# Adjacency masks of a four-layer graph kernel: cast by GpSimd's transfers instead of by ScalarE

## The chip, the cores and the metric

The kernel runs on one core of one Trainium2 chip. The time is the device time of one execution in microseconds. The kernel before has a median of 260.65 us over 3 runs (260.47 to 260.87). The core has five engines that follow their own instruction lists and meet at semaphores: TensorE (PE, with its weight loads shown as PEld), VectorE (DVE), ScalarE (ACT), GpSimd (POOL) and SyncE (SP), which here only issues transfers.

## The reference, cut to what matters

There are 32 graphs of 256 nodes with 128 features each. `adj` is int32 with values 0 and 1 only; it is symmetric and has a full diagonal.

```python
x = _layernorm(x + _L0_gnn_ref(x, adj, W0, a_src, a_dst))   # attention
x = _layernorm(x + _L1_gnn_ref(x, adj, W1, a))              # attention
x = _layernorm(x + _L2_gnn_ref(x, adj, a0, a1, a2, a3, bias))
x = _layernorm(x + _L3_gnn_ref(x, adj3, adj, weight, bias))
# L0 and L1: h = x W^T;  e = leaky_relu(s_i + d_j, 0.2), masked where adj == 0
#            out = softmax(e) h
# L2: alpha = sigmoid(leaky(x a_r x^T)) where adj == r + 1, else 0;  out = alpha x + bias
# L3: out = sum_r (adj == r + 1) x W_r + bias
```

With values 0 and 1 the relation of layers 2 and 3 is always the first one, so one mask per graph serves all four layers. The kernel notes on the way whether a value other than 0 and 1 occurs (step `seen`) and would then compute everything again on a general path, which does not run with these inputs.

## The kernel before

**Units of work.** Two graphs make a pair; there are 16 pairs, numbered 0 to 15. Every step works on one pair. A tile has 128 partitions; a graph's 256 nodes are two blocks of 128.

**Steps of a pair.** Layers 0 and 1 (the digit stands behind the step's name): `h` projects x on TensorE, `logits` copies two columns on VectorE, `gains` and `v` are exponentials on ScalarE, `dT`, `peak`, `top` and `dmax` find the largest logit of the pair, `rows` spreads the gains along rows on TensorE, `weight` (L857) makes the attention weights on VectorE and multiplies them by the mask, `vals` scales the values on ScalarE, `out` aggregates on TensorE, `rsum`, `rinv` and `res` divide and add the residual on VectorE. `stats` (L907), `var`, `pow` (L541, always on GpSimd) and `norm` make the layer norm; in layer 1 `center` stands between. Layer 2: `xT2` transposes on TensorE and is copied on ScalarE, `xTa` is the same tile scaled by a feature vector (on GpSimd at L565 or on ScalarE at L645), `score` is their product, `sigmoid`, `umax` and `alpha` turn it into weights (alpha multiplies by the mask, L865), then `out2`, `res2` (L888) and the norm. Layer 3: `high` and `low` split x in two f16 parts, `agg` multiplies them by the mask on TensorE, `out3` multiplies by the centred weights, then `res3`, `stats3`, `var3`, `pow3`, `norm3` and the store. `bias` (L536) adds the centred bias to x ahead of `res2` and `res3`.

**Masks before.** SyncE loads the int32 adjacency of a pair into one of four places (`adj_all`, ADJ = 4). ScalarE casts each graph to bf16, times EDGE = 0.5 (`make_mask`, L609), into one of ten places (`mask_all`, MASK = 10), and reads the int32 tile again in `seen` (L601), which takes the square of the value less 0.5 and sums it. The factor 0.5 is wanted by layer 2 (tanh instead of a sigmoid) and is taken out of layer 3 by doubling the centred weights (L762). A load of adjacency waits until the mask and the `seen` of the pair four before it are done.

**Order.** The order of each engine's steps is written out by hand in the table `ORDER`, as pairs `step:pair`, one string per engine ("sp" for SyncE). Where a step can run on two engines, it runs on the one whose string names it (`doer`). `BANKS` gives the bank of PSUM of each product. Engines are in order, so a step that waits holds all behind it. Tiles are rings with a depth in pairs (X_IN 4, XT_IN 3 for the loads of x and its transpose). Step `centre` on VectorE centres weights and biases. In the profile `w_pack` is the first weight matrix with the vectors of all layers beside it.

## Time and profile before

| | us |
|---|---|
| median of 3 runs | 260.65 (260.47 to 260.87) |
| the profiled execution | 259.62 |
| its span in the profile | 257.1 |
| TensorE matmuls busy | 228.6 |
| VectorE busy | 226.5 |
| ScalarE busy | 206.5 |
| GpSimd busy | 173.6 |
| HBM read, written | 17.17 MB, 4.19 MB |

Busy time is the time in which at least one instruction of the engine runs, so it is below the number of instructions times their mean duration where instructions overlap. In the rows further down a group has its busy time first and the mean duration of one instruction behind it. "L857" is a line of the kernel; the name left of the arrow is written, the names right of it are read. "idle before" is time in which the engine stood still just before such an instruction, with the instruction that ended the wait. PEclk is the clock of TensorE that was granted, 1.00 being all of it; DMA is the busy share of the 16 transfer engines.

### The profile page before, as it was taken

How to read it: one execution, taken by the hardware profiler on the slowest of the kernel's cores; microseconds unless marked ns; L12 is line 12 of the kernel's file. 1: busy time of each engine (PE TensorE's matmuls, PEld its weight loads, DVE VectorE, ACT ScalarE, POOL GpSimd, SP SyncE). 2: the span in 40 equal slices, each digit the busy share in tenths (PEclk: the TensorE clock that was granted, in tenths of full speed). 3: DMA queues.
4: the chain of work that ended last, by engine and by line, in shares of the span. 5: the costliest groups of instructions: out<-in, count | busy, mean ns of one | idle time of the engine just before them, and what ended most of it. 6: DMA issues, size and time to landing. Idle time of an engine off the chain costs nothing.

```text
span 257.1 us, 5794 instructions
## 1 busy us (share of the span) xinstructions
PE 228.6 (89%) x1745; PEld 207.1 (81%) x1745; DVE 226.5 (88%) x794; ACT 206.5 (80%) x634; POOL 173.6 (67%) x248
## 2 busy tenths in 40 slices
PE   6869898998988999999999999999999988989670
PEld 6769788986977999879898888898979877887560
DVE  0498999989998999989999999999989998998851
ACT  3797999986867999878359965986895959989874
POOL 1003031759789988697357999867596876799892
PEclk9999999999999999999999999999999997999995
DMA  6997538400020444111142000101100011110113
GB/s 243 402 387 213 209 92 259 166 18 0 1 85 0 126 124 134 71 41 46 41 125 82 3 1 0 42 4 51 34 0 3 3 42 42 42 41 0 43 41 129
DMA packets 12145, 21.77 MB, mean 85 GB/s; under 512 B 1104, under 2 KB 5968, under 8 KB 12112
## 3 DMA queue, kind: packets, MB, share of 16 engines
q1 hardware_dynamic: 11824, 21.24, 24.9%
q8 instruction: 15, 0.25, 0.4%
q10 hardware_dynamic: 288, 0.14, 0.2%
q14 instruction: 18, 0.15, 0.2%
HBM read 17.17 MB, written 4.19 MB: 83 GB/s over the span
## 4 chain that ended last, share of the span: by engine, by line
PE 35%; DVE 23%; ACT 19%; POOL 13%; issue 6%; DMA 1%; POOLq 0%; DVEq 0%; ACTq 0%
PE banks L1176 13%; PE banks L1116 6%; POOL frstd L541 6%; DVE wgt_all L857 5%; DVE fstats L907 5%; PE banks L1143 4%; ACT odd_square L601 4%; POOL fxTa L565 4%; ACT xs_all L678 3%; PE banks L1173 3%; PE banks L1153 3%; DVE fres_all L899 3%; ACT wgt_all L651 3%; PE banks L1133 2%; ACT vals_all L636 2%
## 5 line engine op out<-in xcount | busy, mean ns | idle before, releaser
L541 POOL TENSOR_TENSOR frstd<-fvar,minus_half 128x4 f32<-128x4 f32 x64 | 65.1, 1020 | 36.5 <-ACT fvar L684 29.3
L1176 PE MATMUL banks<-vals_all,wgt_all 128*128 128x129 f32 x512 | 64.0, 279 | 3.4 <-issue 2.5
L1176 PEld LDWEIGHTS banks<-vals_all,wgt_all 128*128 128x128 f32 x512 | 60.6, 194 | 5.1 <-issue 3.1
L857 DVE SCALAR_TENSOR_TENSOR wgt_all<-banks,gain,mask_all 128x256 f32<-128x256 f32 x128 | 52.7, 471 | 1.9 <-PE banks L1133 1.9
L536 POOL TENSOR_TENSOR xb_all<-xs_all,bias_cen 128x256 f32<-128x256 f32 x64 | 45.5, 736 | 8.7 <-ACT xs_all L678 4.0
L907 DVE BATCH_NORM_STATS2 fstats<-fres_all 128x6 f32<-128x256 f32 x128 | 47.8, 417 | 0.5
L678 ACT ACTIVATE xs_all<-fres_all,frstd 128x128 f32<-128x128 f32 x124 | 39.5, 399 | 6.1 <-POOL frstd L541 6.0
L1143 PE MATMUL banks<-fxT,fxTa 128*128 128x256 f32 x128 | 31.3, 386 | 1.8 <-DVE wgt_all L865 0.6
L1176 PE MATMUL banks<-xs_all,wgt_all 128*128 128x128 f32 x256 | 31.4, 276 | 0.4 <-DVE wgt_all L865 0.4
L1176 PEld LDWEIGHTS banks<-xs_all,wgt_all 128*128 128x128 f32 x256 | 29.9, 192 | 0.9 <-DVE wgt_all L865 0.4
L565 POOL TENSOR_SCALAR fxTa<-fxT,w_pack 128x256 f32<-128x256 f32 x28 | 25.6, 930 | 6.4 <-ACT fxT L616 6.4
L1143 PEld LDWEIGHTS banks<-fxT,fxTa 128*128 128x128 f32 x128 | 22.6, 190 | 6.0 <-issue 1.6
L616 ACT COPY fxT<-banks 128x256 f32<-128x256 f32 x64 | 20.4, 382 | 5.7 <-PE banks L1101 4.6
L888 DVE TENSOR_TENSOR fres_all<-banks,xb_all 128x512 f32<-128x512 f32 x32 | 21.6, 678 | 3.4 <-PE banks L1173 3.1
L651 ACT ACTIVATE wgt_all<-banks 128x512 f32<-128x512 f32 x32 | 19.2, 600 | 6.5 <-PE banks L1143 6.4
L821 DVE TENSOR_TENSOR banks<-banks,wgt_all 128x512 f32<-128x512 f32 x32 | 21.0, 688 | 1.4 <-ACT banks L652 1.3
L1153 PE MATMUL banks<-mask_all,fxTa 128*128 128x256 bf16 x128 | 17.3, 276 | 4.3 <-POOL fxTa L547 2.2
L1133 PE MATMUL banks<-ident,gain 128*128 128x128 f32 x128 | 20.1, 284 | 0.9 <-ACT gain L620 0.8
L609 ACT ACTIVATE mask_all<-adj_all 128x512 bf16<-128x512 int32 x32 | 18.4, 630 | 2.6 <-DMA adj_all<-adj_turned 2.5
L865 DVE SCALAR_TENSOR_TENSOR wgt_all<-banks,mask_all 128x512 f32<-128x512 f32 x32 | 20.4, 677 | 0.0
L1116 PE MATMUL banks<-w_fast,xT_all 128*128 128x130 f32 x128 | 19.8, 307 | 0.5 <-DVE w_fast L750 0.3
L547 POOL TENSOR_TENSOR fxTa<-xs_all,fxTa 128x256 f16<-128x256 f32 x30 | 19.6, 678 | 0.0
(90 smaller groups left out, 421.5 us busy)
## 6 DMA issues: line engine op xcount, KB each, us to landing
adj_all<-adj_turned SPq DMA_DIRECT2D x16, 512.0 KB, 4.1
xT_all<-x_turned SPq DMA_DIRECT2D x16, 256.0 KB, 3.0
x_all<-x_laid SPq DMA_DIRECT2D x16, 256.0 KB, 3.7
out<-xs_all SPq DMA_DIRECT2D x16, 256.0 KB, 2.2
bias<-biases_laid SPq DMA_DIRECT2D x1, 128.0 KB, 7.7
w_pack<-W_and_columns ACTq DMA_DIRECT2D x1, 68.0 KB, 2.8
w_fast<-W_turned ACTq DMA_DIRECT2D x1, 64.0 KB, 3.1
w_nat<-in_L_gnn_W SPq DMA_DIRECT2D x1, 64.0 KB, 7.5
```

The source lines that it names most:

```text
L536: nc.gpsimd.tensor_tensor(xb(u)[:, :, :], xs(u)[:, :, :], bias_cen[:, int(l) - 2, :, :], ALU.add).then_inc(fast_pool[k], 1)
L541: nc.gpsimd.tensor_tensor(frstd[:, int(l), slot(n), :], fvar[:, int(l), slot(n), :], minus_half[:, :, :], ALU.pow).then_inc(fast_pool[k], 1)
L565: nc.gpsimd.tensor_scalar(fxTa(u)[:, :], fxT(u)[:, :], a2[:, 0:1], None, ALU.mult).then_inc(fast_pool[k], 1)
L651: nc.scalar.activation(wgt(u), scored, ACT.Tanh, scale=0.5 * SLOPE)
L678: last = nc.scalar.activation(xs(u)[:, b, :], fres(u)[:, b, :], ACT.Copy, scale=frstd[:, int(l), u, b:b + 1])
L857: last = nc.vector.scalar_tensor_tensor(out=wgt(u)[:, c, :], in0=place(f"rows{l}", u), scalar=gain[:, u, c, 1:2], in1=maskT(u)[:, c, :], o ...
L907: nc.vector.bn_stats(fstats[:, u, :, :].rearrange("p b k -> p (b k)"), fres(u)[:, :, :].rearrange("p b d -> p d b")).then_inc(fast_dve[k], 1)
L1116: last = nc.tensor.matmul(place(f"h{l}", u)[:, b * HC:(b + 1) * HC], (xT_in if l == "0" else fxT)(u)[:, b * P:(b + 1) * P], w_fast[:, int( ...
L1133: last = nc.tensor.transpose(place(f"rows{l}", u)[:, b * P:(b + 1) * P], gain[:, u, b, 0:1].to_broadcast([P, P]), ident[:, :])
L1143: last = nc.tensor.matmul(place("score", u)[:, c * N:(c + 1) * N], fxTa(u)[:, c * P:(c + 1) * P], fxT(u)[:, :], start=True, stop=True)
L1153: last = nc.tensor.matmul(place("agg", u), part(u)[:, c, :], maskT(u)[:, c, :], start=c == 0 and part is hi, stop=c == NB - 1 and part is lo)
L1176: last = nc.tensor.matmul(place(f"out{l}", u)[:, b * width:(b + 1) * width], wgt(u)[:, c, b * P:(b + 1) * P], (vals if l in "01" else xs)( ...
```

## The change

The int32 tiles `adj_all` go. A new step `mask` on GpSimd issues a transfer per pair that reads int32 from HBM and writes bf16 into `mask_all`, which now has 16 places, one for each pair. Each has a semaphore of its own. `seen` reads the bf16 mask. The factor 0.5 goes as well: `res2` multiplies by 0.5 and `res3` by 1.0 in the instruction that adds the bias, and the doubling of the centred weights goes.

Work changes engines by the table: xTa was on GpSimd for 14 pairs and on ScalarE for 14 and 15; now it is on GpSimd for the pairs 0, 2, 4, 6, 8, 10 and 12 and on ScalarE for the other nine. The layer 1 norms were on GpSimd for nine pairs and on ScalarE for seven; now they are ten and six. The bias sums of bias2:1 and bias3:14 are on VectorE; the layer 2 norm of VectorE was pair 11 and is pair 15; low:15 goes from VectorE to GpSimd. All orders and all banks are new.

On GpSimd the start of the program was this (the identity matrix, then variances and the powers of layers 0 and 1 for the first pairs):

```order
L525 AFFINE_SELECT ident<-zero 128x128
L541 TENSOR_TENSOR frstd<-fvar,minus_half 128x4 x2
L571 TENSOR_SCALAR fvar<-fstats 128x4
L541 TENSOR_TENSOR frstd<-fvar,minus_half 128x4
L571 TENSOR_SCALAR fvar<-fstats 128x4
L541 TENSOR_TENSOR frstd<-fvar,minus_half 128x4
L571 TENSOR_SCALAR fvar<-fstats 128x4
L541 TENSOR_TENSOR frstd<-fvar,minus_half 128x4 x2
```

and is now this (the transfers are of all 16 pairs):

```order
L511 AFFINE_SELECT ident<-zero 128x128
L515 DMA mask_all<-adj_turned 128x1024 x16
L560 TENSOR_SCALAR fvar<-fstats 128x4
L530 TENSOR_TENSOR frstd<-fvar,minus_half 128x4
L560 TENSOR_SCALAR fvar<-fstats 128x4
L530 TENSOR_TENSOR frstd<-fvar,minus_half 128x4
L560 TENSOR_SCALAR fvar<-fstats 128x4
L530 TENSOR_TENSOR frstd<-fvar,minus_half 128x4 x3
L525 TENSOR_TENSOR xb_all<-xs_all,bias_cen 128x256 x2
L544 TENSOR_SCALAR xs_all<-fres_all,frstd,fcenter 128x128 x4
```

All transfers stand in front of the first variance and the first power. On ScalarE the start, up to the values of pair 0 and a little on, was this:

```order
L609 ACTIVATE mask_all<-adj_all 128x512 x2
L620 ACTIVATE gain<-logit 128x8
L601 ACTIVATE odd_square,odd<-adj_all,minus_half 128x1024
L626 ACTIVATE vals_all<-logit,minus_dmax 128x4
L609 ACTIVATE mask_all<-adj_all 128x512 x2
L636 ACTIVATE vals_all<-banks,vals_all 128x128 x4
L620 ACTIVATE gain<-logit 128x8
L601 ACTIVATE odd_square,odd<-adj_all,minus_half 128x1024
L620 ACTIVATE gain<-logit 128x8
L609 ACTIVATE mask_all<-adj_all 128x512 x2
```

and is now this (L592 is `seen`, L604 `gains`, L610 `v`, L620 `vals`, L600 the copies of xT1):

```order
L592 ACTIVATE odd_square,odd<-mask_all,minus_half 128x1024
L604 ACTIVATE gain<-logit 128x8 x2
L592 ACTIVATE odd_square,odd<-mask_all,minus_half 128x1024
L604 ACTIVATE gain<-logit 128x8
L610 ACTIVATE vals_all<-logit,minus_dmax 128x4 x2
L620 ACTIVATE vals_all<-banks,vals_all 128x128 x8
L592 ACTIVATE odd_square,odd<-mask_all,minus_half 128x1024
L610 ACTIVATE vals_all<-logit,minus_dmax 128x4
L620 ACTIVATE vals_all<-banks,vals_all 128x128 x4
L592 ACTIVATE odd_square,odd<-mask_all,minus_half 128x1024
L600 COPY fxT_0<-banks 128x256
L600 COPY fxT_1<-banks 128x256
```

`seen` of pair 0 is now the first instruction, `seen` of pair 2 is the third step, and three pairs go side by side. On VectorE, from the first logits to the first residual, it was this:

```order
L830 COPY logit<-banks 128x4 x2
L838 TENSOR_REDUCE top<-banks 4x1
L842 TENSOR_REDUCE minus_dmax<-banks 128x1
L857 SCALAR_TENSOR_TENSOR wgt_all<-banks,gain,mask_all 128x256 x4
L830 COPY logit<-banks 128x4 x4
L857 SCALAR_TENSOR_TENSOR wgt_all<-banks,gain,mask_all 128x256 x4
L838 TENSOR_REDUCE top<-banks 4x1
L872 TENSOR_SCALAR frow<-banks 128x2 x2
L880 RECIPROCAL finv<-frow 128x4
L842 TENSOR_REDUCE minus_dmax<-banks 128x1
L857 SCALAR_TENSOR_TENSOR wgt_all<-banks,gain,mask_all 128x256 x4
L899 SCALAR_TENSOR_TENSOR fres_all<-banks,finv,x_all 128x128 x4
```

and is now this (L805 logits, L813 peak, L817 dmax, L831 weights, L846 row sums, L874 the residual):

```order
L805 COPY logit<-banks 128x4 x4
L831 SCALAR_TENSOR_TENSOR wgt_all<-banks,gain,mask_all 128x256 x4
L813 TENSOR_REDUCE top<-banks 4x1 x2
L805 COPY logit<-banks 128x4 x2
L817 TENSOR_REDUCE minus_dmax<-banks 128x1 x2
L813 TENSOR_REDUCE top<-banks 4x1
L831 SCALAR_TENSOR_TENSOR wgt_all<-banks,gain,mask_all 128x256 x8
L846 TENSOR_SCALAR frow<-banks 128x2 x2
L817 TENSOR_REDUCE minus_dmax<-banks 128x1
L854 RECIPROCAL finv<-frow 128x4
L874 SCALAR_TENSOR_TENSOR fres_all<-banks,finv,x_all 128x128 x4
```

The weights of pairs 2 and 1 moved ahead of the row sums of pair 0, and the logits of pair 1 ahead of the weights of pair 0.

The diff, with the bodies of the tables cut:

```diff
@@ -54,125 +54,122 @@
-X_IN, XT_IN, ADJ, MASK, XS, FXT, FXTA, VALS, WGT, SG, FRES, XB = 4, 3, 4, 10, 6, 7, 5, 6, 7, 2, 9, 5
-EDGE = 0.5
+X_IN, XT_IN, MASK, XS, FXT, FXTA, VALS, WGT, SG, FRES, XB = 4, 3, 16, 6, 7, 5, 6, 7, 2, 9, 5
...
-        "mask:0 gains0:0 seen:0 v0:0 mask:1 vals0:0 gains0:1 seen:1 gains0:2 mask:2 seen:2 v0:1 mask:3 vals0:1 seen:3 "
+        "seen:0 gains0:0 gains0:1 seen:2 gains0:2 v0:0 v0:1 vals0:0 vals0:1 seen:1 v0:2 vals0:2 seen:3 xT1:0 seen:5 "
...
-        "pow0:0 pow0:1 var0:2 pow0:2 var0:3 pow0:3 var0:4 pow0:4 pow1:0 norm1:0 bias2:0 pow0:5 xTa:0 pow1:1 bias2:1 "
+        "mask:0 mask:2 mask:1 mask:3 mask:5 mask:8 mask:15 mask:6 mask:4 mask:11 mask:10 mask:14 mask:7 mask:9 mask:12 "
+        "mask:13 var0:0 pow0:0 var0:1 pow0:1 var0:2 pow0:2 pow1:0 pow1:1 bias2:0 norm1:1 xTa:0 pow1:2 norm1:2 bias2:2 "
...
@@ -217,7 +214,7 @@
 UP_SQUARE = UP * UP
-COUNTS = {"pe": counts("pe", apart=("turn",)), "act": counts("act"), "dve": counts("dve", apart=("centre",)), "pool": counts("pool")}
+COUNTS = {"pe": counts("pe", apart=("turn",)), "act": counts("act"), "dve": counts("dve", apart=("centre",)), "pool": counts("pool", apart=("mask",))}
 def at(engine, name, u):
@@ -322,7 +319,7 @@
         wait_carrier = sb("wait_carrier", [P, K + 1])
         x_all = sb("x_all", [P, X_IN * H, NB, D])
-        adj_all = sb("adj_all", [P, ADJ * H, NB, N], I32)
+        adj_i = sb("adj_i", [P, NB, N], I32)
         xT_all = sb("xT_all", [P, XT_IN * H, N])
         mask_all = sb("mask_all", [P, MASK * H, NB, N], BF16)
         xs_all = sb("xs_all", [P, XS * H, NB, D])
@@ -416,7 +409,7 @@
         w0_turned_in = sem("w0_turned_in")
         weights_in = sem("weights_in")
         biases_in = sem("biases_in")
-        fast_adj_in = [sem(f"fast_adj_in_{q}") for q in range(ADJ)]
+        fast_mask_in = [sem(f"fast_mask_in_{q}") for q in range(TEAMS)]
         fast_xT_in = [sem(f"fast_xT_in_{q}") for q in range(XT_IN)]
         fast_x_in = [sem(f"fast_x_in_{q}") for q in range(X_IN)]
         fast_pe = [sem(f"fast_pe_{k}") for k in range(K)]
@@ -462,13 +455,6 @@
         @block.sync
         def _(sp):
-            def load_adj(l, n, k):
-                if n >= ADJ:
-                    masker = doer("mask", n - ADJ)
-                    sp.wait_ge(signals[masker][(n - ADJ) % K], at(masker, "mask", final(n - ADJ)))
-                    sp.wait_ge(fast_act[(n - ADJ) % K], at("act", "seen", (n - ADJ) * H))
-                sp.dma_start(adj_all[:, pair(n, ADJ), :, :], adj_turned[n]).then_inc(fast_adj_in[n % ADJ], 16)
-
             def load_x(l, n, k):
                 if n >= X_IN:
                     sp.wait_ge(fast_dve[(n - X_IN) % K], at("dve", "res0", final(n - X_IN)))
@@ -525,6 +511,9 @@
             nc.gpsimd.affine_select(out=ident[:, :], in_=zero[:, :], compare_op=ALU.not_equal, fill=1.0,
                                     base=0, pattern=[[-1, P]], channel_multiplier=1).then_inc(ident_set, 1)
             pool.wait_ge(ident_set, 2)
+            def cast_mask(l, n, k):
+                nc.gpsimd.dma_start(mask_all[:, pair(n, MASK), :, :], adj_turned[n]).then_inc(fast_mask_in[n], 16)
+
             def biases(l, n, k):
                 pool.wait_ge(bias_cen_set, 4)
                 normer = doer(f"norm{int(l) - 1}", n)
@@ -594,19 +583,14 @@
             SEEN = [n for step, l, n in order("act") if step == "seen"]
             def note_odd(l, n, k):
-                act.wait_ge(fast_adj_in[n % ADJ], loaded(n * H, ADJ))
-                if SEEN.index(n):
+                act.wait_ge(fast_mask_in[n], 16)
+                if not SEEN.index(n):
+                    act.wait_ge(ident_set, 2)
+                else:
                     m = SEEN[SEEN.index(n) - 1]
                     act.wait_ge(fast_act[m % K], at("act", "seen", m * H))
-                nc.scalar.activation(odd_square[:, :, :, :], adj_all[:, pair(n, ADJ), :, :], ACT.Square, bias=minus_half[:, 0, 0:1],
+                nc.scalar.activation(odd_square[:, :, :, :], mask_all[:, pair(n, MASK), :, :], ACT.Square, bias=minus_half[:, 0, 0:1],
                                      accum_out=odd[:, n:n + 1]).then_inc(fast_act[k], 1)
-
-            def make_mask(l, n, k):
-                if n >= MASK:
-                    act.wait_ge(fast_pe[(n - MASK) % K], at("pe", "agg", final(n - MASK)))
-                act.wait_ge(fast_adj_in[n % ADJ], loaded(n * H, ADJ))
-                for u in graphs(n):
-                    nc.scalar.activation(maskT(u)[:, :, :], adj_in(u)[:, :, :], ACT.Copy, scale=EDGE).then_inc(fast_act[k], 1)
             def copy_xT(l, n, k):
                 act.wait_ge(fast_pe[k], at("pe", f"xT{l}", final(n)))
@@ -758,8 +742,6 @@
             def output_centre():
                 dve.wait_ge(weights_in, 16)
                 center(1, w3_cen[:, :], w3[:, 0, :], w3[:, 0, :], w3_cen_set)
-                dve.wait_ge(w3_cen_set, 1)
-                nc.vector.tensor_scalar(w3_cen[:, :], w3_cen[:, :], 1 / EDGE, None, ALU.mult).then_inc(w3_cen_set, 1)
             def bias_centres():
                 dve.wait_ge(biases_in, 16)
@@ -848,8 +823,7 @@
             def weights(l, n, k):
                 dve.wait_ge(fast_pe[k], at("pe", f"rows{l}", final(n)))
                 if l == "0":
-                    masker = doer("mask", n)
-                    dve.wait_ge(signals[masker][k], at(masker, "mask", final(n)))
+                    dve.wait_ge(fast_mask_in[n], 16)
                     if n >= WGT:
                         dve.wait_ge(fast_pe[(n - WGT) % K], at("pe", "out2", final(n - WGT)))
                 for u in graphs(n):
@@ -885,7 +859,8 @@
                     dve.wait_ge(signals[biaser][k], at(biaser, f"bias{l}", final(n)))
                     dve.wait_ge(fast_pe[k], at("pe", f"out{l}", final(n)))
                     gathered = banks[:, bank_of(f"out{l}", n * H), :].rearrange("p (h b c) -> p h b c", h=H, b=NB)
-                    nc.vector.tensor_tensor(fres_all[:, pair(n, FRES), :, :], gathered, xb_all[:, pair(n, XB), :, :], ALU.add).then_inc(fast_dve[k], 1)
+                    nc.vector.scalar_tensor_tensor(out=fres_all[:, pair(n, FRES), :, :], in0=gathered, scalar={"2": 0.5, "3": 1.0}[l],
+                                                   in1=xb_all[:, pair(n, XB), :, :], op0=ALU.mult, op1=ALU.add).then_inc(fast_dve[k], 1)
                     return
                 for u in graphs(n):
                     if l == "0" and n >= FRES:
@@ -1156,7 +1131,7 @@
             def outputs(l, n, k):
                 if l == "3" and n == first("pe", "out3"):
-                    pe.wait_ge(w3_cen_set, 2)
+                    pe.wait_ge(w3_cen_set, 1)
                 for u in graphs(n):
                     if l in "01" or u % H == 0:
                         bank_free(f"out{l}", u)
```

## Rows read from the trace of the kernel before

**Rows 1.** The page, part 1: busy us, share of the span, instructions

```profile
PE 228.6 (89%) x1745; PEld 207.1 (81%) x1745; DVE 226.5 (88%) x794; ACT 206.5 (80%) x634; POOL 173.6 (67%) x248
```

**Rows 2.** Stages: length, busy us (instructions) of PE, PEld, DVE, ACT, POOL, PEclk, DMA, GB/s

```profile
0.00:33.40 33.40, 27.68 (x187) 25.26 (x188) 21.99 (x102) 25.36 (x68) 3.16 (x11) 1.00 0.79 280
33.40:241.20 207.80, 194.26 (x1511) 176.81 (x1509) 197.93 (x678) 170.32 (x529) 159.35 (x224) 0.99 0.18 55
241.20:257.10 15.90, 6.62 (x50) 4.99 (x50) 6.60 (x16) 10.86 (x38) 11.04 (x15) 0.82 0.20 69
```

**Rows 3.** Waits of VectorE, 33.4 to 241.2 us: releaser, us, times, longest

```profile
DVE minus_dmax L842 <- PE banks L1126: 1.5, 3, 0.8
DVE banks L821 <- ACT banks L652: 1.3, 4, 0.4
DVE fcenter L921 <- POOL frstd L541: 1.3, 3, 0.6
...
DVE fscale L846 <- ACT vals_all L626: 0.4, 1, 0.4
DVE bad L929 <- ACT xs_all L675: 0.4, 1, 0.4
```

**Rows 4.** Groups by line and shape: count, busy us, mean ns, idle before

```profile
L565 POOL TENSOR_SCALAR fxTa<-fxT,w_pack 128x256 f32<-128x256 f32 x28 | 25.6, 930 | 6.4 <-ACT fxT L616 6.4
...
L888 DVE TENSOR_TENSOR fres_all<-banks,xb_all 128x512 f32<-128x512 f32 x32 | 21.6, 678 | 3.4 <-PE banks L1173 3.1 <-PE banks L1176 0.3
...
L865 DVE SCALAR_TENSOR_TENSOR wgt_all<-banks,mask_all 128x512 f32<-128x512 f32 x32 | 20.4, 677 | 0.0
...
L609 ACT ACTIVATE mask_all<-adj_all 128x512 bf16<-128x512 int32 x32 | 18.4, 630 | 2.6 <-DMA adj_all<-adj_turned 2.5
...
L555 POOL TENSOR_SCALAR xs_all<-fres_all,frstd,fcenter 128x128 f32<-128x128 f32 x36 | 15.8, 455 | 5.1 <-DVE fcenter L921 5.1
...
L645 ACT ACTIVATE fxTa<-banks,w_pack 128x256 f32<-128x256 f32 x4 | 1.7, 492 | 0.0
...
L794 DVE TENSOR_TENSOR fxTa<-xs_all,fxTa 128x256 f16<-128x256 f32 x2 | 0.8, 422 | 0.8 <-ACT fxTa L658 0.8
```

**Rows 5.** Timeline, 1 to 21 us: start, us, engine, line, operation

```profile
1.18 0.29 POOL L525 TENSOR_SCALAR_AFFINE_SELECT ident<-zero 128x128 f32<-128x128 f32 x1 [0.20 <-POOL zero L522]
1.20 0.91 SPq L470 DMA_DIRECT2D adj_all<-adj_turned  x2
...
4.86 2.10 PE L1116 MATMUL banks<-w_fast,xT_all 128*128 128x130 f32 x8 [0.32 <-DVE w_fast L750]
5.42 1.15 ACT L609 ACTIVATE mask_all<-adj_all 128x512 bf16<-128x512 int32 x2 [2.49 <-DMA adj_all<-adj_turned]
...
8.23 1.11 PE L1133 MATMUL banks<-ident,gain 128*128 128x128 f32 x4
...
9.38 1.66 DVE L857 SCALAR_TENSOR_TENSOR wgt_all<-banks,gain,mask_all 128x256 f32<-128x256 f32 x4 [0.89 <-PE banks L1133]
...
11.49 1.13 ACT L601 ACTIVATE odd_square<-adj_all,minus_half 128x1024 bf16<-128x1024 int32 x1
...
17.32 1.12 DVE L899 SCALAR_TENSOR_TENSOR fres_all<-banks,finv,x_all 128x128 f32<-128x128 f32 x4
...
18.55 0.75 DVE L907 BATCH_NORM_STATS2 fstats<-fres_all 128x6 f32<-128x256 f32 x2
...
19.70 1.03 POOL L541 TENSOR_TENSOR frstd<-fvar,minus_half 128x4 f32<-128x4 f32 x1 [18.22 <-ACT fvar L684]
```

**Rows 6.** DMA issues by line: count, KB each, median us to landing

```profile
adj_all<-adj_turned SPq DMA_DIRECT2D x16, 512.0 KB, 4.1
```

**Rows 7.** Stages again, the second of 8 us

```profile
8.00:16.00 8.00, 7.80 (x48) 7.38 (x48) 4.86 (x19) 6.75 (x18) 0.00 (x0) 1.00 1.05 386
```

**Rows 8.** Timeline, the last layer 2 residual

```profile
241.21 0.67 DVE L888 TENSOR_TENSOR fres_all<-banks,xb_all 128x512 f32<-128x512 f32 x1
```

17 lines of the change are left out of this document (4 added, 13 removed), and 191 rows, old and new, of tables (BANKS, ORDER).

## The prediction

> **What bounds the kernel now.** I read three views first. The page's busy shares come first: TensorE and VectorE are both near nine tenths [rows 1], and the question is which of the two has slack. The reader is to take the seconds behind the shares. VectorE's sum is 226.5 us. TensorE's matmuls are pipelined, and the page says a busy PE is not one at its peak; VectorE's instructions are not stretched like this. The second view is the table by stages [rows 2]. VectorE is busy 21.99 of the first 33.40 us, 197.93 of the next 207.80, and 6.60 of the last 15.90. So its 30.6 us of idle time are 11.4 at the start, 9.9 in the long middle and 9.3 in the tail. ScalarE has 170.32 of 207.80 in the middle and GpSimd 159.35. The third view is who keeps VectorE waiting in the middle [rows 3]: TensorE's small transposes for 1.5 us, and ScalarE and GpSimd, in four rows, for 1.3 + 1.3 + 0.4 + 0.4 = 3.4 us.
>
> So work taken from ScalarE or GpSimd is worth nothing by itself: it pays only as far as it removes idle time of VectorE. The end is a sum: VectorE's idle time before the last layer 2 residual, its work up to there, and a latency chain behind it. That residual starts at 241.21 [rows 8], and the 15.9 us behind it hold 6.60 us of VectorE work [rows 2]: dependent steps of the last pairs, not load.
>
> **The change part by part.** (1) The 32 casts of masks on ScalarE go: 18.4 us [rows 4]. ScalarE takes seven more pairs of xTa, 14 instructions at 1.7/4 = 0.43 us, 6.0 us. Net it is relieved of 12.4 us. (2) GpSimd loses these seven pairs: 14 of the 28 instructions that cost 25.6 us, so 12.8 us, and gets one more pair of layer 1 norms, 4 x 0.44 = 1.8 us (15.8/36) [rows 4]. Net it has 11 us less, before what the 16 transfers cost it. (3) VectorE: two pairs of bias sums come to it, 4 instructions at 0.4 us (the row of two that read two f32 tiles there) = 1.6 us. One small multiplication of the output weights goes. The pair of layer 2 norms done by VectorE was pair 11 and becomes pair 15: four 128x128 operations, some 1.1 us by the four of the residual [rows 5], leave the body for the tail, where they replace ScalarE's norm on the chain. Body: 1.6 - 1.1 less the small one is some 0.3 us; one step of the low parts leaves it too, and I put the body at 0. (4) The residuals of layers 2 and 3 become a multiply-and-add: 32 x 678 ns now against 677 ns for the three-operand form of the same 128x512 [rows 4]. Zero. (5) The low part of pair 15 goes from VectorE to GpSimd; in the tail before, the last pair's low part was already on GpSimd, so zero.
>
> (6) The start, walked in the new order with the durations of [rows 5]. The first projection starts at 4.86 and takes 2.1 us, the second ends near 9.1 (all matmuls are slow at this point although the clock column of the stage reads 1.00 [rows 7]; I keep the slow figure for both). Then the rows of pair 0 (1.1), the third projection, the rows of pair 2: VectorE can do the layer 0 weights of pair 0 from 10.0 to 11.7, waits for TensorE until about 14.5, does those of pairs 2 and 1 (1.66 each) until 17.8, the first residual (1.12) until 19.5, statistics (0.75) until 20.4, then weight centres, two residuals and statistics until 25.2, where logits1:0 stands. Up to there it has 3 x 1.66 + 3 x 1.12 + 2 x 0.75 of these and some 4.7 of small steps, 14.5 us of work, so 10.7 of idle time. Before, 11.4 us of idle time lie ahead of 33.40 [rows 2]; I leave 0.1 for small gaps between 25.2 and there. Gain 0.6 us. Behind logits1:0 both orders have enough pairs at hand to keep it busy.
>
> (7) GpSimd's 16 transfers. They stand in a row ahead of its first variance (the rows of GpSimd's order in the section on the change); GpSimd is in order, so behind them wait var0:0 and pow0:0, for these VectorE's logits1:0, and behind that everything on VectorE. GpSimd is free from 1.5 us (the affine select ends at 1.47 [rows 5]) and pow0:0 with the variance ahead of it takes some 1.2 (1.03 of it the power), so it must be through with the transfers by 24.0: (24.0 - 1.5)/16 = 1.41 us each. No row shows such an issue on GpSimd. Bounds: 0.46 us each from SyncE's two in 0.91 us [rows 5], sum 7.4 us; and 4.1 us, the time from issue to landing of the same tile [rows 6], were GpSimd held until each has landed, sum 65.6 us. Its nearest row is the small operation of 1.03 us, since every instruction of GpSimd in the trace pays something like it. I take 1.1 us: 17.6 us, through at 19.1, hidden with 4.9 us to spare. Ends of the cost: 0, and 1.5 + 65.6 - 24.0 = 43 us.
>
> Here a rule of the Trainium skill speaks against the change. The row shows that SyncE's issue is short and that nothing of VectorE bears on it. The skill (SBUF — State Buffer, section on the "DVE blocks DMA" trap) says that descriptors of a GpSimd transfer are written by GpSimd's own cores, and that they are locked out while VectorE runs a two-port operation from SBUF to SBUF. No run here shows it yet. By it the sum would grow by the few such operations of the start, one cast and the weight centres, under 1 us of GpSimd's time, which the 4.9 us to spare would swallow.
>
> (8) The transfers' data. Before, the first adjacency was there at 5.42 after 4.2 us [rows 5]. Now ScalarE's first instruction, seen:0, waits for mask:0 and stands ahead of gains0:0 and gains0:1; gains0:1 can't run before 9.0, so mask:0 may land up to about 7.4 us (seen takes 1.13, the reading of its sum and gains0:0 a little more). That is 5.9 us after it can be issued: enough at 4.2. Later, twelve seen: steps stand ahead of v0:3 (about 31 us). Twelve masks are 6.3 MB of reading, and x and xT up to then some 2.9 MB; at the 386 GB/s of [rows 7] that is 24 us. Enough, if a casting transfer runs at the rate of a plain one; at half that rate for the masks it is (12.6 + 2.9)/0.386 = 40 us, 9 to 10 us late.
>
> (9) The middle. Masks stand resident from the start, so no load waits for ScalarE, and both helpers have more slack: 170.3 - 12 of 207.8 on ScalarE, 159.4 - 11 on GpSimd. The gain lies between 0 and the 9.9 us that VectorE is idle there. I take the 3.4 us that rows put down to ScalarE and GpSimd [rows 3]; TensorE's share stays.
>
> Sum: -0.6 - 3.4 + 0 = -4.0 us. Against the profiled execution, 259.62 us with a span of 257.1, this is 255.6; the median of the runs is 260.65, 1.0 above the profiled one, and so the forecast is 256.7 us.
>
> **The rivals.** (A) Slower: GpSimd's issues hold the first power. It decides from 1.41 us each. At 1.8 us the last is done at 30.3, 6.3 us after the deadline, VectorE has nothing ahead of logits1:0, and -4.0 + 6.3 = +2.3 us: 263. At 1.66 the whole gain is eaten. For it: all 16 stand at the head, and GpSimd is slow at everything in the trace (1.03 us for 128x4). Against it: it only needs to write lists.
> (B) Slower: the data come late because a cast halves the rate. ScalarE then stands at seen: steps and not at work; v0:3 comes 9 to 10 us late. VectorE can fill perhaps half of it with layer 1 of pairs 0 to 2, so +5 - 4 = +1 us or more: 262 to 266. Against it: half the bytes are written.
> (C) No change: idle time of VectorE in the middle is TensorE's doing, as ScalarE and GpSimd were only the last of several signals. Then start and middle give 0.6 or less, and 260.3 comes out. For it: TensorE is at 194.26 of 207.80 in the same stage [rows 2]. The order is a new one throughout, so idle time can also appear elsewhere.
> (D) It goes better: both the start and half of TensorE's waits go as well, -7 us: 253.7.
>
> **How the numbers follow.** Forecast, with 254.5 to 259.5 of its own: 0.50. D 0.08. C 0.14, of which half within 0.2% (0.5 us, about what a measurement of this kernel can tell from no change), the rest split. A 0.18, B 0.10. Faster by over 0.2%: 0.50 + 0.08 + 0.04 = 0.62. Within it: 0.08. Slower: 0.28 + 0.02 = 0.30. The range from 253.5 takes in D; above, it goes to 264.5, which holds C, most of A up to 1.9 us each, and half of B.
>
> **What would show it.** In the changed profile: GpSimd's first variance starts at once when the first statistics are done, near 20 us (right), or GpSimd is still issuing then (A). ScalarE's seen: row with idle time released by the transfers above 5 us shows B. VectorE's busy sum stays within 2 us of 226.5, and its idle time from 33 us to the last layer 2 residual falls from 9.9 to about 6.5; if it stays, C. ScalarE's busy sum falls to some 194 us and GpSimd's to some 163 plus what the profile counts of the issues. The tail from that residual to the end stays near 16 us. The forecast is wrong if the tail grows, for I have no term for it, or if the multiply-and-add costs more than 678 ns.

## The result, and the profile after the change

Five runs of the changed kernel gave 258.22, 256.33, 250.7, 252.42 and 254.5 us, median 254.5, beside 260.65 (260.19 to 261.16) before: a ratio of 0.965 (0.961 to 0.969). Six more of the same kernel gave a median of 254.47 (252.15 to 256.85), ratio 0.974 (0.971 to 0.977). Over all eleven the median is 6.2 us below that of before. The forecast was 4.0 us below, so the sign held and the size did not: the gain is half as large again by the medians, 1.7 times by the ratio of the repeat (some 6.8 us) and more than twice by the first (some 9.1 us). The ratios, here and below, leave out runs in the slower of two states of the chip, three of the first five and one of the repeat, while medians and ranges are of all runs. The spread is new too: eleven runs lie within 7.5 us, where 22 runs of before lie within 1.8.

The profiled execution read here is that of the repeat, 254.96 us with a span of 253.1. Against 259.62 and 257.1 before that is -4.7 us, of it -4.0 in the span and -0.7 around it.

Ahead of the rows, one correction. The prediction took the residual at 241.21 us [rows 8] for the last one of layer 2. By VectorE's written order the low part of pair 15 follows the layer 3 residual of pair 13, and in the trace it follows the one at 241.21. The last layer 2 residual (of pair 12, by the order before) is the one ahead of it:

```profile
239.81 0.69 DVE L888 TENSOR_TENSOR fres_all<-banks,xb_all 128x512 f32<-128x512 f32 x1 [0.28 <-PE banks L1176]
```

So the long middle of before ends at 239.81, not at 241.21. The stages cut there, first before, then after (its last layer 2 residual is at 235.05); columns as in [rows 2]:

```profile
33.40:239.81 206.41, 193.48 (x1506) 176.22 (x1505) 196.57 (x676) 169.69 (x527) 157.96 (x222) 0.99 0.18 55
239.81:257.10 17.29, 7.41 (x58) 5.58 (x56) 7.96 (x18) 11.49 (x41) 12.43 (x17) 0.84 0.19 64
```

```profile
0.00:33.40 33.40, 28.02 (x185) 24.73 (x186) 21.84 (x102) 20.82 (x57) 13.10 (x29) 1.00 1.03 237
33.40:235.05 201.65, 191.35 (x1507) 176.13 (x1507) 195.32 (x675) 162.40 (x528) 146.84 (x207) 1.00 0.14 41
235.05:253.10 18.05, 6.79 (x57) 5.53 (x55) 7.98 (x21) 9.70 (x34) 9.66 (x13) 0.76 0.22 75
```

VectorE is the third pair of numbers. Its idle time at the start is 33.40 - 21.84 = 11.56 us (11.41 before), in the middle 201.65 - 195.32 = 6.33 (before 9.84). Its work up to the last layer 2 residual is 21.84 + 195.32 = 217.16 (before 218.56), and the tail behind it is 0.76 longer. The four differences are +0.15, -3.51, -1.40 and +0.76: together -4.0. (After the change the last layer 2 residual is that of pair 15, so the two tails do not hold the same steps in the same order.)

Busy sums after, beside [rows 1]:

```profile
PE 226.2 (89%) x1745; PEld 206.4 (82%) x1745; DVE 225.1 (89%) x795; ACT 192.9 (76%) x616; POOL 169.6 (67%) x248
```

Waits of VectorE from 33 to 240 us after: the two rows on GpSimd's power and on the value scales [rows 3] are gone, and a bias sum that VectorE now does itself waits for ScalarE's norm instead. Over all rows of this view, cut at the last layer 2 residual, the waits for ScalarE and GpSimd fell from 3.4 us to 2.2 and those for TensorE from 4.4 to 2.0.

```profile
DVE frow L846 <- PE banks L1151: 1.1, 2, 0.8
DVE banks L796 <- ACT banks L636: 0.8, 3, 0.3
DVE bad L904 <- ACT xs_all L662: 0.7, 1, 0.7
DVE xb_all L763 <- ACT xs_all L662: 0.7, 1, 0.7
```

The groups that answer to [rows 4] (count, busy us, mean ns, idle before):

```profile
L862 DVE SCALAR_TENSOR_TENSOR fres_all<-banks,xb_all 128x512 f32<-128x512 f32 x32 | 21.5, 676 | 1.9 <-PE banks L1148 1.9
L839 DVE SCALAR_TENSOR_TENSOR wgt_all<-banks,mask_all 128x512 f32<-128x512 f32 x32 | 20.4, 677 | 0.0
...
L544 POOL TENSOR_SCALAR xs_all<-fres_all,frstd,fcenter 128x128 f32<-128x128 f32 x40 | 17.5, 453 | 5.8 <-DVE fcenter L896 5.8
L554 POOL TENSOR_SCALAR fxTa<-fxT,w_pack 128x256 f32<-128x256 f32 x14 | 13.1, 943 | 1.9 <-ACT fxT L600 1.9
...
L515 POOL DMA_DIRECT2D mask_all<-adj_turned x16 | 8.7, 623 | 0.3 <-POOL ident L511 0.3
...
L629 ACT ACTIVATE fxTa<-banks,w_pack 128x256 f32<-128x256 f32 x18 | 7.8, 498 | 0.0
...
L763 DVE TENSOR_TENSOR xb_all<-xs_all,bias_cen 128x256 f32<-128x256 f32 x4 | 2.1, 546 | 0.7 <-ACT xs_all L662 0.7
```

The multiply-and-add residual costs 676 ns, not more than the plain addition. Two groups of small VectorE instructions changed their mean although nothing about them was edited, variances (`fvar`) and value scales (`fscale`); each pair of rows has before first:

```profile
L913 DVE SCALAR_TENSOR_TENSOR fvar<-fstats,fvar 128x4 f32<-128x4 f32 x16 | 4.3, 270 | 0.0
L888 DVE SCALAR_TENSOR_TENSOR fvar<-fstats,fvar 128x4 f32<-128x4 f32 x16 | 2.5, 155 | 0.1
L846 DVE TENSOR_TENSOR fscale<-vals_all,frstd 128x4 f32<-128x4 f32 x16 | 4.6, 287 | 0.4 <-ACT vals_all L626 0.4
L821 DVE TENSOR_TENSOR fscale<-vals_all,frstd 128x4 f32<-128x4 f32 x16 | 6.0, 377 | 0.0
```

The median of one is 0.15 to 0.16 us in all four. The kernel before had long ones too: one `fscale` took 1.20 us and three `fvar` 0.63 to 0.69. The experiment "One input or two" comes back to this. The timeline of the start (beside [rows 5]) shows the transfers:

```profile
1.79 8.72 POOL L515 DMA_DIRECT2D mask_all<-adj_turned  x16 [0.31 <-POOL ident L511]
...
4.87 2.10 PE L1091 MATMUL banks<-w_fast,xT_all 128*128 128x130 f32 x8 [0.32 <-DVE w_fast L734]
...
8.81 1.15 ACT L592 ACTIVATE odd_square<-mask_all,minus_half 128x1024 bf16<-128x1024 bf16 x1 [5.81 <-DMA mask_all<-adj_turned]
...
9.88 0.23 DVE L805 COPY logit<-banks 128x4 f32<-128x4 f32 x2 [2.64 <-PE banks L1091]
...
11.36 1.66 DVE L831 SCALAR_TENSOR_TENSOR wgt_all<-banks,gain,mask_all 128x256 f32<-128x256 f32 x4 [1.25 <-PE banks L1108]
...
20.46 0.20 POOL L560 TENSOR_SCALAR fvar<-fstats 128x4 f32<-128x4 f32 x1 [9.95 <-DVE fstats L882]
```

GpSimd issued all 16 in 8.72 us, 0.54 us each, and then stood idle for 9.95 us until VectorE's first statistics: it was never late, and rival (A) is out. But ScalarE stood for 5.81 us at its first instruction, and did the first gains only behind it, at 9.96. Over the whole execution ScalarE waited 6.2 us for masks, 5.81 and 0.40 of it at its first two `seen`, and never again. The issue row and the stage of 8 us that answer to [rows 6, 7]:

```profile
mask_all<-adj_turned POOLq DMA_DIRECT2D x16, 256.0 KB, 15.9
```

```profile
8.00:16.00 8.00, 7.41 (x43) 6.34 (x44) 4.17 (x17) 5.03 (x17) 2.51 (x5) 1.00 1.11 251
```

A transfer of 256 KB written (512 KB read) lands 15.9 us after its issue (median) when 16 are queued at once, where a plain one took 4.1. The DMA engines are busy all through these 8 us and move 251 GB/s as counted, where it was 386. But the profile counts a cast by the bytes that it writes: 4.20 MB for the queue of the 16, while 17.17 MB are read from HBM before and after. Of the 2.01 MB counted in these 8 us the casts are 1.16 MB; counted as the int32 that they read it is 3.17 MB, 396 GB/s. So the casts read as fast as the plain loads did.

### The profile page after: what moved, and what is told of

Read it like the earlier page. It is cut to its first block, busy times and chain, and to the rows that moved or that the text cites. A ratio compares the mean times of both kernels' runs of the same rounds, so it can differ in the third digit from the quotient of the medians.

```text
span 256.3 us, 5743 instructions
## 1 busy us (share of the span) xinstructions
PE 231.5 (90%) x1745; PEld 212.4 (83%) x1745; DVE 224.1 (87%) x795; ACT 193.0 (75%) x616; POOL 169.2 (66%) x248
## 3 DMA queue, kind: packets, MB, share of 16 engines
HBM read 17.17 MB, written 4.19 MB: 83 GB/s over the span
## 4 chain that ended last, share of the span: by engine, by line
PE 45%; DVE 35%; ACT 10%; issue 4%; DMA 3%; POOL 1%; DVEq 0%; ACTq 0%; POOLq 0%
PE banks L1151 23%; DVE wgt_all L831 8%; DVE fstats L882 6%; PE banks L1091 6%; DVE fres_all L874 5%; PE banks L1118 4%; PE banks L1076 3%; PE banks L1108 3%; DVE fres_all L862 3%; DMA mask_all<-adj_turned 3%; DVE banks L796 3%; PE banks L1148 2%; ACT xs_all L662 2%; DVE wgt_all L839 2%; ACT wgt_all L635 2%
## 5 line engine op out<-in xcount | busy, mean ns | idle before, releaser
L1151 PE MATMUL banks<-vals_all,wgt_all 128*128 128x129 f32 x512 | 66.5, 288 | 0.3 <-DVE wgt_all L839 0.2
L1151 PEld LDWEIGHTS banks<-vals_all,wgt_all 128*128 128x128 f32 x512 | 63.8, 203 | 1.4 <-DVE wgt_all L839 0.5
L831 DVE SCALAR_TENSOR_TENSOR wgt_all<-banks,gain,mask_all 128x256 f32<-128x256 f32 x128 | 52.5, 470 | 4.0 <-PE banks L1108 4.0
L525 POOL TENSOR_TENSOR xb_all<-xs_all,bias_cen 128x256 f32<-128x256 f32 x60 | 42.3, 728 | 10.0 <-ACT xs_all L662 7.7
L1118 PE MATMUL banks<-fxT,fxTa 128*128 128x256 f32 x128 | 30.6, 382 | 1.3 <-ACT fxTa L629 1.2
L600 ACT COPY fxT<-banks 128x256 f32<-128x256 f32 x64 | 20.7, 379 | 12.8 <-PE banks L1076 9.1
L592 ACT ACTIVATE odd_square<-mask_all,minus_half 128x1024 bf16<-128x1024 bf16 x16 | 18.6, 1165 | 6.9 <-DMA mask_all<-adj_turned 6.7
L862 DVE SCALAR_TENSOR_TENSOR fres_all<-banks,xb_all 128x512 f32<-128x512 f32 x32 | 21.5, 676 | 1.9 <-PE banks L1148 1.9
L536 POOL TENSOR_TENSOR fxTa<-xs_all,fxTa 128x256 f16<-128x256 f32 x32 | 21.2, 685 | 1.9 <-ACT fxTa L642 1.9
L544 POOL TENSOR_SCALAR xs_all<-fres_all,frstd,fcenter 128x128 f32<-128x128 f32 x40 | 17.4, 447 | 7.3 <-DVE fcenter L896 7.2
L1091 PE MATMUL banks<-w_fast,xT_all 128*128 128x130 f32 x128 | 20.7, 312 | 1.2 <-DVE wgt_all L831 0.8
L620 ACT ACTIVATE vals_all<-banks,fscale 128x128 f32<-128x128 f32 x64 | 18.4, 383 | 3.9 <-DVE fscale L821 3.9
## 6 DMA issues: line engine op xcount, KB each, us to landing
w_nat<-in_L_gnn_W SPq DMA_DIRECT2D x1, 64.0 KB, 12.4
```

Of the source, the lines that this page charges most:

```text
L525: nc.gpsimd.tensor_tensor(xb(u)[:, :, :], xs(u)[:, :, :], bias_cen[:, int(l) - 2, :, :], ALU.add).then_inc(fast_pool[k], 1)
L831: last = nc.vector.scalar_tensor_tensor(out=wgt(u)[:, c, :], in0=place(f"rows{l}", u), scalar=gain[:, u, c, 1:2], in1=maskT(u)[:, c, :], o ...
L862: nc.vector.scalar_tensor_tensor(out=fres_all[:, pair(n, FRES), :, :], in0=gathered, scalar={"2": 0.5, "3": 1.0}[l], in1=xb_all[:, pair(n, ...
L1091: last = nc.tensor.matmul(place(f"h{l}", u)[:, b * HC:(b + 1) * HC], (xT_in if l == "0" else fxT)(u)[:, b * P:(b + 1) * P], w_fast[:, int( ...
L1118: last = nc.tensor.matmul(place("score", u)[:, c * N:(c + 1) * N], fxTa(u)[:, c * P:(c + 1) * P], fxT(u)[:, :], start=True, stop=True)
L1151: last = nc.tensor.matmul(place(f"out{l}", u)[:, b * width:(b + 1) * width], wgt(u)[:, c, b * P:(b + 1) * P], (vals if l in "01" else xs)( ...
```

## The experiments

Theories 1 to 3 of the expectations are that the relief pays by itself, that the order does, and that the share of xTa taken from GpSimd does. Theory 4 came up with the late masks: ScalarE's early seen: steps stand in the way. Theories 5 and 6 are told where they are tested.

**The change again.** No edit.

> The changed kernel once more, for a profile of an undisturbed execution. Theory 1 (helpers): VectorE's idle time in the middle falls well under the 8.8 us of the first profile, with ScalarE and GpSimd gone from the list of what VectorE waits for. Theory 2 (order): idle time in the middle falls too, but by TensorE's waits. Both: about 251 to 252 us, idle time at the start about 2.4 us above before.

254.47 us, as told above. The profile is the one just read.

**The cast alone, in the old order.**

```diff
 sp:   - adj:0 ... adj:15
 act:  - mask:0 ... mask:15
 pool: + mask:0 mask:1 ... mask:15 (ahead of pow0:0)
```

> One part of the change alone: masks cast by GpSimd's transfers at the head of its order, all else (orders, banks, who does xTa and norms) as before. Theory 1 (the 18.4 us taken from ScalarE are what pays): 3 to 6 us faster than before, 255 to 257.5. Theory 2 (only the new order pays): within 1.5 us of before, 259 to 262, since this order was made around ScalarE's casts; a late first mask can cost up to 3 us of that.

260.89 us, ratio 1.001 (0.999 to 1.003): nothing. ScalarE has 18 us less to do, and it is worth nothing. In the profile VectorE does less than before from 16 to 32 us (first row; second, before):

```profile
16.00:32.00 16.00, 11.94 (x82) 10.50 (x82) 11.73 (x52) 7.33 (x25) 2.06 (x2) 0.89 1.11 251
```

```profile
16.00:32.00 16.00, 13.31 (x106) 11.99 (x106) 14.77 (x71) 14.04 (x43) 2.04 (x2) 1.00 0.75 252
```

The 3 us lost there are not given back: every later residual of layers 2 and 3 is 2 to 3 us behind its place before. But this profile is of the slowest of the twelve runs, 262.77 us. The kernel of the next experiment has the same transfers and the same orders up to there, and in its profile (259.03 us, the fastest of its twelve) the stretch is nearly that of before:

```profile
16.00:32.00 16.00, 12.80 (x101) 11.32 (x101) 14.35 (x66) 10.41 (x35) 2.06 (x2) 1.00 1.11 253
```

So the 3 us belong to that execution, and they do not explain why the median gains nothing.

**The cast and the shares, in the old order.** As the last, and xTa of seven pairs from GpSimd to ScalarE.

```diff
 act:  + xTa:1 (behind xT2:1), the same for 3, 5, 7, 9, 11, 13
 pool: - xTa:1, 3, 5, 7, 9, 11, 13
```

> The old order with cast transfers (run a1, 260.9 us) and in addition xTa of the pairs 1, 3, 5, 7, 9, 11 and 13 on ScalarE, right behind the copy of xT2: both engine shares of the change (nearly), none of its order. Theory 3 (what pays is GpSimd's relief of 12.8 us, made possible by ScalarE's casts going; run a3 gave back 9.5 us when it was undone): 255 to 258. Theory 2 (only the order that was made for it pays): 259.5 to 262.

260.32 us, 0.998 (0.996 to 1.000). Relieving both helpers pays nothing, or 0.6 us, in the old order: theories 1 and 3 fall as they stand.

**The order alone.** The new order and banks; int32 loads by SyncE and casts by ScalarE as before.

```diff
 sp:   + adj:0 ... adj:15 (behind xT:0 ... xT:15)
 act:  + mask:n, seen:n ahead of or behind gains0:n
 pool: - mask:0 ... mask:15
```

> The other part alone: the new orders and banks with the masks cast by ScalarE as before (int32 tiles loaded by SyncE, four places; mask and seen of a pair around its gains0). ScalarE has 12.4 us less relief. Theory 1: near before or slower, 259 to 266, as ScalarE's casts stand in the first layers' way. Theory 2 (the order carries the gain): 253 to 257.

264.33 us, 1.015 (1.012 to 1.018). Alone the order costs 3.8 us, so theory 2 falls as well; with the relief it gains 6.2. One thing more differs, though: with the int32 tiles in four places, `seen` of a pair has to stand near its `gains0`, so most `seen` steps of this kernel are in the middle and not in the first 40 us. Further down that alone cost 4.4 us, so how much of the 3.8 us is the order's own is not shown. The two profiles are level early (first layer 2 residual at 53.26 and 53.19 us). Behind 60 us they part; first the order alone, then with the cast, up to the last layer 2 residual:

```profile
60.00:242.56 182.56, 168.47 (x1312) 152.99 (x1311) 171.80 (x578) 156.06 (x494) 130.27 (x185) 1.00 0.16 53
```

```profile
60.00:235.05 175.05, 166.04 (x1310) 152.77 (x1310) 170.29 (x579) 137.25 (x455) 128.69 (x182) 1.00 0.12 37
```

VectorE is idle for 182.56 - 171.80 = 10.8 us in the one and 4.8 in the other, and ScalarE has 156.06 us of 182.56 against 137.25 of 175.05.

**ScalarE loaded again.** 32 copies of a mask to scratch, the size of the casts.

```diff
 act:  + extra:n (behind gains0:n, n = 0 ... 15)
+nc.scalar.activation(scratch_all[:, u % 2, :, :], maskT(u)[:, :, :], ACT.Copy, scale=0.5)
```

> The changed kernel with the removed load put back on ScalarE: 32 copies of 128x512 (bf16 in, bf16 out, into a scratch tile that nobody reads) right behind gains0 of each pair, some 18.5 us in all. Theory 1: gives back most, 256 to 262. Theory 2: ScalarE has slack in the new order, at most 2 us slower than the changed kernel, 251 to 254.

261.33 us (257.8 to 264.5), 0.998 (0.994 to 1.001): 6.9 us of the gain go with ScalarE's time alone by the medians, some 6 by the ratios (0.998 against 0.974). Where they are lost the profiles do not show. In this one, 258.86 us, the first layer 2 residual is at 57.27 against 53.19, but the first profile of the changed kernel, without any load put back, has it at 57.73.

**xTa of seven pairs back on GpSimd.**

```diff
 act:  - xTa:1, 3, 5, 7, 9, 11, 13
 pool: + xTa:1 (behind norm1:1), xTa:3 (behind bias2:3), the same for 5 to 13
```

> The changed kernel with xTa of the pairs 1, 3, 5, 7, 9, 11 and 13 put back on GpSimd (0.93 us each instead of 0.5 on ScalarE), behind the bias sums of the pair. GpSimd gets 12.8 us, ScalarE loses 6. Theory 1: 2 to 4 us slower than the changed kernel, since GpSimd's in-order chain of powers is delayed. Theory 2: within 1 us.

263.98 us, 1.010 (1.007 to 1.014): 9.5 us worse for 13 us of GpSimd's work. VectorE's waits show one way in which it comes (the first row had no counterpart in the changed kernel from 33 us on):

```profile
DVE fcenter L897 <- POOL frstd L531: 4.0, 3, 2.2
DVE minus_dmax L818 <- PE banks L1102: 2.7, 2, 1.4
DVE banks L797 <- ACT banks L637: 2.6, 6, 1.0
```

**Half of the transfers later.** Three kernels: eight at the head and eight one by one behind the first powers (seen in the order of the transfers); the same with ScalarE's two first gains ahead of seen:0; and the old order with six at the head and ten behind powers.

```diff
 pool: - mask:8 ... mask:15 (head)   + mask:8 (behind pow0:0) ... mask:15 (behind pow2:0)
 act:  - seen:0 gains0:0 gains0:1    + gains0:0 gains0:1 seen:0      (second only)
```

> The changed kernel with the transfers staged: masks 0, 2, 1, 3, 4, 5, 6, 7 at GpSimd's head, the other eight one by one behind its first powers; seen: steps at the same places, in the order of the transfers. Theory A (16 transfers at once take the bandwidth of the first x and xT and of masks 0 to 2, which moves the start about from run to run): 1 to 4 us faster than the changed kernel (median 254.5), and less spread. Rival (the start waits for TensorE's slow beginning, not for data): within 1 us.

> As b1, and on ScalarE gains0:0 and gains0:1 ahead of seen:0, so that the first rows of TensorE do not wait for the first mask. Theory A: another 0.5 to 2 us below b1 (seen:0 began at 8.8 and 9.2 us in two profiles of the changed kernel, and took 1.3). Rival: the same as b1, since VectorE's first weights need the mask anyway.

> The old order with cast transfers (run a1, 260.9 us), six at GpSimd's head and the other ten one by one behind its first powers. Theory 1 (relief of ScalarE pays by itself, and a1 lost it to late masks in the start): 256 to 258.5. Theory 2 (relief alone gives nothing behind the start, it needs an order that uses it): 259.5 to 261.5, with the milestones behind 70 us at a constant distance from before.

272.41, 269.93 and 271.18 us: 1.040, 1.035 and 1.042, all far from what I expected. Issues and median landing in the first of them, the eight at the head, then the eight single ones:

```profile
mask_all<-adj_turned POOLq DMA_DIRECT2D x8, 256.0 KB, 11.8
```

```profile
mask_all<-adj_turned POOLq DMA_DIRECT2D x8, 256.0 KB, 3.8
```

A single cast lands in 3.8 us, no slower than the plain load of 512 KB. But an issue behind a power waits as long as that power does (the eight single ones are issued between 22.2 and 64.7 us), the mask comes late, and ScalarE, which is in order, stands at seen:. Waits of ScalarE in the same kernel:

```profile
ACT odd_square L594 <- DMA mask_all<-adj_turned: 18.9, 5, 6.0
```

All 16 ahead of anything that waits was better than each of these three stagings, even with 15.9 us to landing. Nor does a shorter queue bring the first mask earlier: ScalarE's first instruction starts at 9.02 us with eight transfers at the head, and at 8.81 and 9.21 us in the two profiles with sixteen.

**Seen later, and the transposed x first.** On the changed kernel, one on top of the other.

```diff
 act:  - seen:0 gains0:0 gains0:1    + gains0:0 gains0:1 seen:0
 sp:   - xT:0 x:0 xT:1 xT:2 x:1      + xT:0 xT:1 xT:2 x:0 weights:0 x:1   (second only)
```

> The changed kernel, ScalarE's start only: gains0:0 and gains0:1 ahead of seen:0, so that TensorE's first rows do not wait for the first mask. Theory A (the late first mask costs by this wait): 1 to 2 us faster than the changed kernel, 252.5 to 253.5. Rival (VectorE's first weights need the mask anyway): within 0.7 us.

> As c2, and SyncE loads xT of the pairs 0, 1 and 2 ahead of every x (x is first needed by the first residual near 18 us, xT of pair 1 was waited for at 7.7 us in a profile). Theory A (the first us are bound by what the 16 transfers leave of the bandwidth): another 0.5 to 2 us and a smaller spread than 250.7 to 258.2. Rival: no change, as TensorE's slow beginning sets the pace.

252.92 us (0.969, 0.966 to 0.973) and 251.57 us (249.6 to 257.0; 0.961, 0.958 to 0.965). The late mask at ScalarE's head costs about 1.5 us by the medians, and in the profile of the first kernel each residual of layers 2 and 3 is 1.5 us ahead of its place in the profile of the changed kernel. But the intervals of the ratios (0.966 to 0.973 here, 0.971 to 0.977 in the repeat) overlap, and the two profiles of the changed kernel itself are 4.5 us apart at the first such residual, so the 1.5 us are likely, not shown. The second is the best kernel of this study that computes all. How much the SyncE order adds is not settled, by what follows two experiments on.

**Seen spread over the middle.** On top of that, 12 seen: steps moved behind agg: and norm3: steps.

```diff
 act:  - seen:5 (behind xT1:0) ...   + seen:5 (behind agg:0), seen:8 (behind agg:1), ... seen:9 (behind agg:8)
```

> As c3, and twelve of the sixteen seen steps (1.36 us of ScalarE each) leave the first 40 us and are spread over the middle. Theory 4 (ScalarE's load in the start is what costs; the 18.5 us put back in a2 cost 7, of which 4.1 were there at the first layer 2 residual): 2 to 5 us faster than c3. Rival (a2 lost by the load everywhere): within 1 us of c3, or slower as the middle gets fuller.

255.99 us, 0.981 (0.978 to 0.984): 4.4 us worse, against my expectation. Early, ScalarE has room for these 1.2 us steps; in the middle they stand ahead of steps that VectorE waits for. In this profile the value scales of VectorE wait 2.6 us for ScalarE's `v` behind 33 us, in that of the kernel before it not at all.

**One input or two.** Single executions of one program differ by several us, and the profiles show a part of it. The fscale step of 128x4 near 155 us, in the timeline of the kernel with seen later, with GpSimd's row beside it, and in that of the one with the transposed x first:

```profile
154.55 2.84 DVE L823 TENSOR_TENSOR fscale<-vals_all,frstd 128x4 f32<-128x4 f32 x1
...
153.34 1.42 POOL L527 TENSOR_TENSOR xb_all<-xs_all,bias_cen 128x256 f32<-128x256 f32 x2
```

```profile
154.98 0.22 DVE L823 TENSOR_TENSOR fscale<-vals_all,frstd 128x4 f32<-128x4 f32 x1
...
153.77 1.41 POOL L527 TENSOR_TENSOR xb_all<-xs_all,bias_cen 128x256 f32<-128x256 f32 x2
```

It starts 0.21 and 0.20 us ahead of the end of GpSimd's bias sums, the same moment, and lasts 2.84 us or 0.22. The spans of these two profiles are 251.4 and 249.3, and up to this step the first was the faster by 0.4.

In the changed kernel's profile the same step takes 2.85 us, and it ends with GpSimd's last instruction of an unbroken row (VectorE's timeline, then GpSimd's):

```profile
156.09 2.85 DVE L821 TENSOR_TENSOR fscale<-vals_all,frstd 128x4 f32<-128x4 f32 x1
```

```profile
154.88 1.42 POOL L525 TENSOR_TENSOR xb_all<-xs_all,bias_cen 128x256 f32<-128x256 f32 x2
156.25 1.31 POOL L536 TENSOR_TENSOR fxTa<-xs_all,fxTa 128x256 f16<-128x256 f32 x2
157.51 1.42 POOL L525 TENSOR_TENSOR xb_all<-xs_all,bias_cen 128x256 f32<-128x256 f32 x2
```

156.09 + 2.85 = 158.94 and 157.51 + 1.42 = 158.93. By the Trainium skill (SBUF — State Buffer, "Who interferes with whom") a VectorE instruction with two inputs in SBUF contends with a GpSimd instruction that reads SBUF, and the loser blocks fully. The end of this one agrees with that. But it was held beyond the GpSimd instruction within which it began, over the four behind it as well.

The other profiles say the same. In the 18 profiles of this study VectorE's 128x4 instructions with two inputs in SBUF (`fscale`, `fvar`, `fcenter`) took over 0.4 us 61 times, where the median is 0.15. In 60 of the 61 GpSimd was at a bias sum or a low part when they began, instructions that read two tiles of 128x256, and all 60 ended 12 to 60 ns behind the end of such an instruction. No 128x4 instruction of VectorE with fewer inputs in SBUF took over 0.18 us. The 0.22 us one above fits too: it ended 20 ns behind the bias sum within which it began. The 2.84 us one began at the same point of the same row and was not let in at that end, nor at the next ones. What decides that is open.

The held step is on the path. From the layer 2 residual of pair 7 to that of pair 8, the changed kernel's profile and that of the kernel with the transposed x first:

```profile
149.12 0.66 DVE L862 SCALAR_TENSOR_TENSOR fres_all<-banks,xb_all 128x512 f32<-128x512 f32 x1
...
160.57 0.67 DVE L862 SCALAR_TENSOR_TENSOR fres_all<-banks,xb_all 128x512 f32<-128x512 f32 x1
```

```profile
148.02 0.66 DVE L864 SCALAR_TENSOR_TENSOR fres_all<-banks,xb_all 128x512 f32<-128x512 f32 x1
...
156.91 0.67 DVE L864 SCALAR_TENSOR_TENSOR fres_all<-banks,xb_all 128x512 f32<-128x512 f32 x1
```

11.45 us with the long one and 8.89 without. In the 14 profiles with the new order it is 11.4 to 11.8 us in the five that hold a long one here and 8.9 to 9.1 in the other nine, so the long one costs the execution some 2.5 us.

Two kernels to test it, both without the norm's factor in fscale, so of the same value and the same waits:

```diff
-nc.vector.tensor_tensor(fscale[...], vals_all[..., D], frstd[:, 0, slot(n), :], ALU.mult)
+nc.vector.tensor_reduce(fscale[...], vals_all[..., D:D + 1], AX.X, ALU.max)          (one input)
+nc.vector.tensor_tensor(fscale[...], vals_all[..., D], vals_all[..., D], ALU.max)    (two inputs)
```

> The changed kernel, with fscale (VectorE, 128x4) made as a reduction over one element of the weights' scale alone, so that the instruction reads one tile of SBUF. The factor of the layer norm is left out of it; the output differs by that. In the profile of the changed kernel one such instruction, which reads two tiles, took 2.85 us at 156.1 us and ended with GpSimd's bias sum, another 1.08 us at 114.7; in the first profile of the same kernel the instruction at the same place took 0.2 us. Theory 5, a VectorE instruction with two inputs in SBUF is held while GpSimd works one instruction behind the other: no fscale above 0.3 us here, and the time below that of the two-input form (d4) by 1 to 3 us at the median, with a smaller spread. Theory 6, the long one is an artefact or a semaphore wait: no difference between d1 and d4 (under 0.5 us).

> Partner of d1: the same fscale without the layer norm's factor (the same value and the same waits), but as an element-wise maximum of the tile with itself, so that VectorE reads two inputs in SBUF as in the changed kernel. Theory 5: single instructions of 1 us and of 2.5 to 3 us come back, at the same places (near 115 and 156 us) in most executions; median 254 to 255, as the changed kernel. Theory 6: the two instructions are short here too, since the wait for the power is gone, and the time is that of d1.

One input: 252.67 us (250.25 to 253.9), 0.970 (0.966 to 0.974). Two: 255.88 (252.4 to 258.2), 0.977 (0.971 to 0.982). The medians differ by 3.2 us, the ratios only by some 1.8 us, their intervals overlap, and the one profile of the two-input form holds none above 0.36 us (in both kernels the profiled run is the fastest). So this pair does not decide between theories 5 and 6. The profiles above speak for theory 5 in what is held and until when. The fscale step in the profiles of the one and the other (duration in ns: shortest, median, longest):

```profile
L821 DVE TENSOR_REDUCE fscale<-vals_all x16: 116/146/158, 29.1 to 208.1; 128x4 f32<-128x4 f32 x16
```

```profile
L821 DVE TENSOR_TENSOR fscale<-vals_all x16: 136/152/358, 30.8 to 209.8; 128x4 f32<-128x4 f32 x16
```

> The best version so far (c3_xt_first, 251.57) with the one-input fscale of d1. Its profile held no long fscale, at 251.24 us, though its runs go from 249.6 to 257.0. Theory 5: if the long ones are behind a part of the spread, the median falls to 250 or 251 and what spread is left is that of the start and TensorE's clock. Theory 6: 251.5 with the same spread.

The best version with the one-input form (norm's factor left out): 250.43 us (249.6 to 251.5), 0.963 (0.959 to 0.966). Its six runs lie within 2.0 us, where those of the best version lie within 7.4. But that range comes from two of six runs, and the intervals of the ratios overlap, so neither a gain nor less spread is shown.

**The tail as before.** On the best version, the layer 2 norm of pair 15 back on ScalarE, the layer 3 bias sum of pair 14 back on GpSimd.

```diff
 dve:  - bias3:14 norm2:15
 act:  + norm2:15 (ahead of high:15)
 pool: + bias3:14 (behind pow2:15), pow3:12 behind low:15
```

> c3_xt_first with the last pairs' steps as before the change: the layer 2 norm of pair 15 back on ScalarE (ahead of its high part), the bias sum of pair 14 for layer 3 back on GpSimd, ahead of the low part of pair 15. In the profiles the part behind the last layer 2 residual went from 17.3 us before to 18.05 after the change. If the norm and the bias sum on VectorE are worth it, the end comes 0.5 to 1.5 us later (252 to 253); if they cost what the tail grew by, 0.5 to 1 us earlier (250.5 to 251); with neither on the chain, the same within 0.3.

255.84 us, 0.983 (0.980 to 0.987), 4.3 worse. Its profile holds a fscale of 2.83 us, and that of the best version none, so some 2.5 of it may be that. The tail behind the last layer 2 residual is 19.93 us against 17.92 in the best version: the last residual waits for the slower norm and its successors.

```profile
243.87 0.69 DVE L864 SCALAR_TENSOR_TENSOR fres_all<-banks,xb_all 128x512 f32<-128x512 f32 x1 [4.29 <-PE banks L1150]
```

The steps that VectorE took over at the end are worth 2 us by these two profiles; without them the change would have lost them.

## Why the prediction was wrong in size

The sign was right, and so was the place of the main gain, VectorE's idle time in the middle. The forecast for the profiled execution, 255.6 us against 254.96, came close by luck. Its span was to fall by 4.0 us and fell by 4.0, but of the terms three were off, by -1.4, +0.75 and +0.76 us, and they cancel. Step by step:

- (1), (2) ScalarE's sum fell by 13.6 us (forecast 12.4), GpSimd's by 4.0 with 8.7 us of issues in it, so by 12.7 without them (forecast 11). Right.
- (4) the residual as a multiply-and-add: 676 ns. Right.
- (7) the issues: 0.54 us each, near the lower bound of 0.46, not the 1.1 I took. It changed nothing, since they were hidden at either. The reason given for 1.1, that every instruction of GpSimd pays about a microsecond, was wrong already in [rows 5], where one takes 0.29.
- (9) the middle: -3.5 for a forecast -3.4, but not by the route I gave. I took away the 3.4 us that rows put down to ScalarE and GpSimd and left TensorE's share. Measured, the waits for the two fell by 1.2 us and those for TensorE by 2.4. And in the old order taking that load away gave 0.0 and 0.6 us. It is the relief together with the new order that pays. In the new order ScalarE's share is worth 6 to 7 us and that of xTa 9.5, more than all the waits named in [rows 3]; the new order without the relief is worse than before by 3.8.
- (6), (8) the start: +0.15, not -0.6. mask:0 was wanted by 7.4 and was read at 8.81. I let it land like a lone plain load, 4.2 us after its issue, and it took about 7, with eight in the queue as with sixteen; why the first is late is open. By its letter the sign of rival (B) came up, 6.2 us of waits for masks against the 5 named. But what (B) described did not happen: behind the first two masks ScalarE waited for none, and the casts read at the rate of plain loads. The loss is 0.75 us where (B) had 5. Moving one step past the wait won about 1.5 by the medians.
- The tail: +0.76, with no term in the sum. The prediction named a growing tail as a sign of being wrong. The 15.9 us that it compared with were cut at the wrong residual; rightly cut it is 17.29 before and 18.05 after.
- (3) **the failed step.** I put VectorE's work up to the last layer 2 residual at 0, from counts of instructions times their durations in one trace. It fell by 1.4 us in the paired profiles. The list itself came out as priced, with two small errors that cancel: four bias sums +2.2 us (forecast 1.6), the norm of pair 11 -1.6 (1.1), the small multiplication -0.2, together +0.3. What failed is the assumption that the other instructions keep their durations. The `fvar` steps cost 1.8 us less than before and the `fscale` steps 1.4 us more, since GpSimd held others of them and for longer, and some 0.8 us are instructions that overlap more. In the best version's profile, which has no long `fscale`, VectorE's whole sum is 222.3 us against 225.1. So the work is not a constant of the instruction list. The term is -1.4 us or, with the long one absent, some -4 us.

The same step carries into the last one, from the profiled execution to the median. I carried over that before's median is 1.0 us above its profiled run. After the change the median is 0.5 below its profiled run, one with the long `fscale`, which costs some 2.5 us of path and is not in every execution. That is 1.5 of the 2.2 us between -4.0 and -6.2; the other 0.7 is the time outside the span (1.9 us after, 2.5 before), for which I had no term. That the median lies below because of the long one is argued from the profiles, since unprofiled runs do not show whether they hold it.

What stays open: why the ratio of the first five runs gives -9 us (it rests on two of them, 250.7 and 252.42); how often the long fscale comes (5 of the 11 profiles with the new order and the full fscale have one of over 2.8 us); how much of the order's 3.8 us is the place of the `seen` steps; and the rest of the spread. The changed kernel's first profile is 4.5 us behind the second one by the first layer 2 residual. In it TensorE was granted half of its clock from 34 to 36 us; it had been busy for 1.07 us of the two from 30 and for 1.54 of the two from 32:

```profile
30.00:32.00 2.00, 1.07 (x8) 0.57 (x7) 2.00 (x9) 1.58 (x5) 0.00 (x0) 1.00 1.12 263
32.00:34.00 2.00, 1.54 (x12) 1.28 (x11) 2.00 (x9) 1.39 (x6) 0.00 (x0) 0.94 0.99 204
34.00:36.00 2.00, 2.00 (x11) 2.00 (x10) 1.84 (x14) 2.00 (x7) 0.00 (x0) 0.50 0.41 44
```

The second one has a granted clock of 1.00 up to 235 us. Whether the dip causes the delay or goes with a late start was not tried.

## What to carry to other kernels

Relief of an engine that is not the bound, and the order written for it, can each be worth nothing or less, and the two together 2.4%: measure the four corners before pricing either. When the terms of a sum come out at the forecast total, check them one by one, for they can cancel. Queue transfers that nothing precedes at the head of an in-order engine, and keep every step that waits for their data behind the first steps of the chain. Price an instruction with two on-chip inputs on an engine that works beside GpSimd with a spread, and take a profile of one execution as one sample.

## What the runs showed of the hardware

- A casting transfer of 128x1024 int32 to bf16 costs GpSimd 0.54 us to issue. Sixteen at once keep all DMA engines busy and land after 15.9 us (median), eight at once after 11.8, single ones after 3.8. The profile counts them by the bytes written, 251 GB/s in 8 us with other loads beside them; by the bytes read it is 396, against 386 with plain int32 loads in the same 8 us.
- Whether VectorE can hold back GpSimd's issues is not shown: the 16 took 8.72 us, and VectorE worked only 0.69 us of them.
- A 128x4 VectorE instruction with two inputs in SBUF took 2.84 us or 0.22 us at moments that lie 10 ns apart as seen from GpSimd's work, and in the long case of the changed kernel it ended with GpSimd's unbroken row. Of 61 such instructions over 0.4 us in 18 profiles, 60 ended 12 to 60 ns behind a GpSimd instruction that reads two tiles of 128x256. The long one near 155 us costs the execution some 2.5 us.
